# Maxima in query tiles of 112 rows, one transpose per group, and fewer second-chunk products in a three-attention decoder layer

## The reference, cut to what matters

```python
def attention(q, k, v, causal):            # 16 heads of 32
    scores = einsum('bhqd,bhkd->bhqk', q, k) / sqrt(32)
    if causal:
        scores = where(tril(ones((S, S))), scores, -inf)
    return einsum('bhqk,bhkd->bhqd', softmax(scores, axis=-1), v)

x = layernorm(x + lora_linear(attention(q(x), k(x), v(x), causal=True), wo))
h = ln(x + attention(q(x), k(x), v(x), causal=False))
h = ln(h + attention(q(h), k(ctx), v(ctx), causal=False))
x = layernorm(x + ln(h + ffn(h)))
x = layernorm(x + bit_ffn(x))
```

## Time and profile before

| | |
|---|---|
| median of three runs | 3351.85 us (3346.13 to 3355.16) |
| the profiled execution, first to last instruction | 3352.8 us |
| mean granted TensorE clock | 0.976 |
| PE busy | 3122.7 us (93%), 35500 matmuls |
| DVE busy | 2591.0 us (77%) |
| ACT busy | 2018.2 us (60%) |
| POOL busy | 1227.7 us (37%) |
| DMA | 405.71 MB, 44.5% of the 16 DMA engines' time |

### The profile page before, as it was taken

The page is one execution under the profiler, slowest core; times in us unless marked ns, Lnnn a source line. Parts: engine busy times, 40 slices in busy tenths (PEclk is TensorE's granted clock), DMA queues, the critical chain, the costliest instruction groups (busy, mean ns, idle before and its releaser), DMA issues.

```text
span 3352.8 us, 88599 instructions
## 1 busy us (share of the span) xinstructions
PE 3122.7 (93%) x35500; PEld 2438.7 (73%) x35500; DVE 2591.0 (77%) x4691; ACT 2018.2 (60%) x4586; POOL 1227.7 (37%) x1128
## 2 busy tenths in 40 slices
PE   6998999999999968999999999999979999999996
PEld 4888888878889846777777777777765656565562
DVE  5777788878889757888888888888855666666666
ACT  2665556656677636777777777777763544434342
POOL 0444431126665643344444443434113212222222
PEclk9999999999999988999999999999989999999998
DMA  3566654436554545656556545555342121121212
GB/s 101 161 192 208 193 167 142 147 118 189 173 165 136 162 113 123 140 132 138 133 123 138 135 124 139 128 135 113 87 173 76 45 53 44 50 54 50 55 38 48
DMA packets 445189, 405.71 MB, mean 121 GB/s; under 512 B 270471, under 2 KB 352523, under 8 KB 443630
## 3 DMA queue, kind: packets, MB, share of 16 engines
q1 hardware_dynamic: 444526, 399.78, 44.5%
q10 hardware_dynamic: 256, 0.26, 0.0%
HBM read 239.72 MB, written 109.52 MB: 104 GB/s over the span
## 4 chain that ended last, share of the span: by engine, by line
PE 59%; DMA 13%; DVE 12%; SPq 6%; ACT 5%; issue 3%; POOL 2%; ACTq 0%; POOLq 0%; DVEq 0%
PE at_ps L752 26%; PE at_ps L876 5%; PE at_ps L896 5%; PE at_ps L839 4%; PE at_ps L1404 4%; PE at_ps L1418 3%; DMA causal_spill<-at_proj 3%; PE at_ps L1429 3%; PE at_ps L1383 3%; DMA self_spill<-at_proj 2%; DVE at_mx_cross L964 2%; PE at_ps L781 2%; DMA at_o_raw<-at_values 2%; PE at_ps L851 2%; SPq L708 1%
## 5 line engine op out<-in xcount | busy, mean ns | idle before, releaser
L971 DVE TENSOR_TENSOR at_p<-at_ps,at_p 125x448 f16<-125x448 f32 (+1 forms) x1280 | 779.6, 617 | 167.5 <-ACT at_ps L924 158.6
L923 ACT ACTIVATE at_p<-at_ps 125x448 f16<-125x448 f32 (+1 forms) x1280 | 698.8, 546 | 292.8 <-PE at_ps L876 254.2
L924 ACT ACTIVATE at_ps<-at_ps 125x448 f32<-125x448 f32 (+1 forms) x1280 | 699.4, 546 | 0.0
L964 DVE TENSOR_REDUCE at_mx_cross<-at_ps 128x1 f32<-128x750 f32 x512 | 477.2, 932 | 41.1 <-PE at_ps L839 38.3
L1044 POOL TENSOR_TENSOR at_o_sum<-at_o_raw 128x256 f32<-128x256 f32 x192 | 121.3, 632 | 930.6 <-ACT at_o_raw L930 930.4
L876 PE MATMUL at_ps<-at_stacks 97*112 97x224 f16 (+2 forms) x1792 | 324.6, 257 | 23.2 <-DMA at_stacks<-at_mrow 19.2
L896 PE MATMUL at_ps<-at_values,at_p 112*128 112x33 f16 (+3 forms) x7168 | 317.0, 185 | 12.1 <-ACT at_o_raw L930 6.7
L916 ACT ACTIVATE at_proj<-at_ps 128x448 f16<-128x448 f32 (+2 forms) x320 | 155.1, 485 | 273.7 <-PE at_ps L752 273.2
L1383 PE MATMUL at_ps<-at_xt,at_early 128*128 128x256 f16 x1792 | 303.2, 276 | 7.8 <-ACT at_w_first L1453 4.9
L1452 ACT ACTIVATE at_masks<-at_ps,at_b_cols 128x256 f32<-128x256 f32 x224 | 107.2, 479 | 336.1 <-PE at_ps L1383 336.0
L967 DVE TENSOR_REDUCE at_mx<-at_ps 128x2 f32<-128x448 f32 x512 | 304.4, 610 | 5.7 <-PE at_ps L851 4.0
(11 more groups left out here) (203 smaller groups left out, 6775.6 us busy)
## 6 DMA issues: line engine op xcount, KB each, us to landing
at_x_res<-x SPq DMA_DIRECT2D x124, 256.0 KB, 3.1
cross_spill<-at_proj SPq DMA_DIRECT2D x64, 487.0 KB, 3.1
at_x_rows<-x SPq DMA_DIRECT2D x92, 256.0 KB, 4.5
at_prep<-bit SPq DMA_DIRECT2D x32, 512.0 KB, 4.6
at_early<-ctx SPq DMA_DIRECT2D x32, 512.0 KB, 5.1
at_stacks<-cross_spill SPq DMA_DIRECT2D x64, 243.5 KB, 3.7
causal_spill<-at_proj SPq DMA_DIRECT2D x64, 224.0 KB, 2.0
at_stacks<-causal_spill SPq DMA_DIRECT2D x128, 112.0 KB, 2.3
```

The costliest lines, as they stand in the source:

```text
L923: act.activation(mem.p_hi[0:self.KC, n % 4, :], scores, ACT.Exp, scale=EXP_SCALE)
L924: act.activation(scores, scores, ACT.Exp, scale=EXP_SCALE).then_inc(self.exp_done, 1)
L964: dve.tensor_reduce(self.mx[:, at, t, h:h + 1], mem.ps_qk[:, :, 0:self.KT // 2], AX.XY, ALU.max).then_inc(self.max_done, 1)
L971: dve.tensor_tensor(mem.p_lo[0:self.KC, n % 4, :], mem.ps_st[0:self.KC, self.st_bank(b, g, n), 0:2 * T], mem.p_hi[0:self.KC, n % 4, :], AL ...
```

## The change

Query tiles of the maxima are 112 rows (`QR`), without overlap, in all three attentions. A group's maxima, 112 rows by two tiles by four heads, are turned round by one transpose to eight rows, and `mrow` becomes eight partitions of 112; two DMAs, one for each tile, write the row, so the waits on `mrow_in` count 32. In the causal attention the first maximum tile needs 112 keys, and its other 112 columns are filled with a mask only in the first use of each of the two banks. In causal `scores` the second chunk is computed for the last 128 queries alone, so the exponentials and the subtraction run over 352 columns instead of 448, and `values` leaves out the second chunk for the first query tile. All products left out are with keys that the mask makes zero. The mask for the maxima is one triangle of 112 instead of two tiles.

```diff
--- before.py
+++ after.py
@@ -34,6 +34,7 @@
 GH = P // HD
 G = D // P
 TILES = (0, T - P)
+QR = T // 2
 S_ACT = 16.0
 S_W = 256.0
 UNSPLIT = 1.0 / (S_ACT * S_W)
@@ -338,7 +339,7 @@
         small = masks[:, :].bitcast(F16)
         self.ot = small[:, 0:1792].rearrange("p (i c t) -> p i c t", i=2, c=DC)
         self.mask_eye = small[:, 1792:1920]
-        self.mask_q = small[:, 1920:2368].rearrange("p (t k) -> p t k", t=2)
+        self.mask_q = small[:, 1920:2144]
         self.mask_k = small[0:T // 2, 2368:2816].rearrange("p (c k) -> p c k", c=2)
         self.ct = [space.bitcast(F16).rearrange("p (i c k) -> p i c k", i=2, c=DC)
                    for space in (masks[:, 0:4 * KT_PAD], second[:, 0:4 * KT_PAD])]
@@ -370,7 +371,7 @@
         self.yn_flat = sb("yn", [P, 2 * D])
         self.z, self.yn, self.y = sb("z", [P, 2, D]), self.yn_flat[:, :].rearrange("p (t d) -> p t d", t=2), sb("y", [P, 2, D])
         self.mx = [sb("mx", [P, 6, 2, GH]), sb("mx_cross", [P, 4, 2, GH])]
-        self.mrow = sb("mrow", [GH, 2, T], F16)
+        self.mrow = sb("mrow", [2 * GH, 2, QR], F16)
         self.stats, self.mv = sb("stats", [P, 2, 6]), sb("mv", [P, 2, 2])
         self.ve, self.rstd = sb("ve", [P, 2]), sb("rstd", [P, 2])
         self.neghalf = sb("neghalf", [P, 2])
@@ -463,6 +464,7 @@
         self.QTILES = (2 if self.cross else 1) * GH
         self.PAIRS = self.NCH // 2 * GH
         self.HALF = self.PAIRS // 2
+        self.P_COLS = T + P if self.causal else 2 * T
         self.w_part = mem.weights[index]
         self.stacks, self.values = (mem.cross_stacks, mem.cross_values) if self.cross else (mem.stacks, mem.values)
         self.RING = len(self.stacks)
@@ -711,7 +713,9 @@
             sp.dma_start(to[0:HD, :, T:], heads[:, :, T:width]).then_inc(self.stacked[g % 2], 16)
         elif kind == "row":
             sp.wait_ge(*self.released(kind, b, g))
-            sp.dma_start(self.qs(b, g)[96:97], self.mrow[:, g % 2, :]).then_inc(self.mrow_in[g % 2], 16)
+            for t in range(2):
+                sp.dma_start(self.qs(b, g)[96:97, :, t * QR:(t + 1) * QR], self.mrow[t * GH:(t + 1) * GH, g % 2, :]
+                             ).then_inc(self.mrow_in[g % 2], 16)
         elif kind == "store":
             if self.norm is None:
                 sp.wait_ge(self.yn_done, 2 * b + 2)
@@ -806,9 +810,8 @@
                                                      for t, q0 in enumerate(TILES)])
             elif kind == "row":
                 pe.wait_ge(self.max_done, self.tile(b, g, QTILES))
-                for t, q0 in enumerate(TILES):
-                    last = pe.transpose(mem.ps_proj[0:GH, bank, q0:q0 + P], self.mx[:, self.place(b, g), t, :],
-                                        mem.ident[:, :])
+                last = pe.transpose(mem.ps_proj[0:2 * GH, bank, 0:QR],
+                                    self.mx[0:QR, self.place(b, g), :, :].rearrange("p t h -> p (t h)"), mem.ident[0:QR, 0:QR])
             elif kind in ("y0", "y1"):
                 if b == self.b0:
                     pe.wait_ge(self.first_weights.w_lo_done, 8)
@@ -836,48 +839,43 @@
             if self.cross:
                 h, t = n // 2, n % 2
                 for half in range(2):
-                    last = pe.matmul(mem.ps_qk[:, half, 0:KT // 2], qs[0:96, h, TILES[t]:TILES[t] + P],
+                    last = pe.matmul(mem.ps_qk[0:QR, half, 0:KT // 2], qs[0:96, h, t * QR:(t + 1) * QR],
                                      ks[0:96, h, half * KT // 2:(half + 1) * KT // 2], start=True, stop=True)
             else:
                 wait(pe, self.max_done, self.tile(b, g, n) - 1)
+                bank = mem.ps_qk[0:QR, n % 2, 0:2 * T].rearrange("p (t k) -> p t k", t=2)
+                if self.causal and b == self.b0 and g == 0 and n < 2:
+                    pe.matmul(bank[:, 0, QR:T], mem.mask_eye[:, 0:QR], mem.mask_q[:, QR:T], start=True, stop=True)
                 for t in range(2):
 
-
-                    first = self.causal and t == 0
-                    k0, k1 = (0, T) if not self.causal or t else (0, P)
-                    if first:
-                        pe.matmul(mem.ps_qk[:, n % 2, 0:T], mem.mask_eye, mem.mask_q[:, 0, :],
-                                  start=True, stop=False)
-                    last = pe.matmul(mem.ps_qk[:, n % 2, t * T + k0:t * T + k1],
-                                     qs[0:96, n, TILES[t]:TILES[t] + P], ks[0:96, n, k0:k1],
-                                     start=not first, stop=not self.causal or first)
-                    if self.causal and not first:
-                        last = pe.matmul(mem.ps_qk[:, n % 2, t * T + TILES[t]:t * T + T], mem.mask_eye,
-                                         mem.mask_q[:, t, TILES[t]:T], start=False, stop=True)
+                    keys = QR if self.causal and t == 0 else T
+                    last = pe.matmul(bank[:, t, 0:keys], qs[0:96, n, t * QR:(t + 1) * QR], ks[0:96, n, 0:keys],
+                                     start=True, stop=not self.causal)
+                    if self.causal:
+                        last = pe.matmul(bank[:, t, t * QR:(t + 1) * QR], mem.mask_eye[:, 0:QR], mem.mask_q[:, 0:QR],
+                                         start=False, stop=True)
             last.then_inc(self.qk_full, 1)
         elif kind == "scores":
             qs, ks = self.qs(b, g), self.ks(b, g)
             if n == 0:
-                pe.wait_ge(self.mrow_in[g % 2], 16 * ((G * b + g) // 2 + 1))
+                pe.wait_ge(self.mrow_in[g % 2], 32 * ((G * b + g) // 2 + 1))
                 if self.cross and b == self.b0:
                     pe.wait_ge(self.slots_set, 2 * g + 2)
             m = self.pair(b, g, n)
             wait(pe, self.lo_done, m - ST_RING + 1)
             bank = self.st_bank(b, g, n)
             h, c0 = n // (NCH // 2), 2 * (n % (NCH // 2))
-            for c in (c0, c0 + 1):
-
-
-                first = self.causal and c > 0
-                q0, at = (c * KC if self.causal else 0), (c - c0) * T
-                if first:
-                    pe.matmul(mem.ps_st[0:KC, bank, at:at + T], mem.mask_eye[0:KC, 0:KC], mem.mask_k[:, c, :],
-                              start=True, stop=False)
-                last = pe.matmul(mem.ps_st[0:KC, bank, at + q0:at + T], ks[:, h, c * KC:(c + 1) * KC],
-                                 qs[:, h, q0:T], start=not first, stop=not self.causal or first)
-                if self.causal and not first:
-                    last = pe.matmul(mem.ps_st[0:KC, bank, at:at + KC], mem.mask_eye[0:KC, 0:KC],
-                                     mem.mask_k[:, c, 0:KC], start=False, stop=True)
+            if self.causal:
+                early, late = mem.ps_st[0:KC, bank, 0:T], mem.ps_st[0:KC, bank, T:T + P]
+                pe.matmul(early, ks[:, h, 0:KC], qs[:, h, 0:T], start=True, stop=False)
+                pe.matmul(early[:, 0:KC], mem.mask_eye[0:KC, 0:KC], mem.mask_k[:, 0, 0:KC], start=False, stop=True)
+                pe.matmul(late, mem.mask_eye[0:KC, 0:KC], mem.mask_k[:, 1, T - P:T], start=True, stop=False)
+                last = pe.matmul(late[:, P - KC:P], ks[:, h, KC:T], qs[:, h, KC:T], start=False, stop=True)
+            else:
+                for c in (c0, c0 + 1):
+                    at = (c - c0) * T
+                    last = pe.matmul(mem.ps_st[0:KC, bank, at:at + T], ks[:, h, c * KC:(c + 1) * KC], qs[:, h, 0:T],
+                                     start=True, stop=True)
             last.then_inc(self.st_full, 1)
         elif kind == "values":
             vs = self.vs(b, g)
@@ -890,6 +888,10 @@
             for c in (c0, c0 + 1):
                 for t, q0 in enumerate(TILES):
                     at = (c - c0) * T + q0
+                    if self.causal and c == 1:
+                        if t == 0:
+                            continue
+                        at = T
                     both = [(mem.p_hi[0:KC, n % 4, at:at + P], VW), (mem.p_lo[0:KC, n % 4, at:at + P], HD + 1)]
                     for k, (left, cols) in enumerate(both if c == 0 else both[::-1]):
                         at_h = h % 2 * VW
@@ -906,8 +908,8 @@
             return
         if kind in self.ALL_JOBS and self.by_scalar(kind):
             act.wait_ge(self.proj_full, self.full_index[kind, b, g] + 1)
-            wait(act, self.mrow_in[g % 2], 16 * ((G * b + g) // 2))
-            act.activation(self.mrow[:, g % 2, :], mem.ps_proj[0:GH, self.jobs.bank(kind, b, g), 0:T], ACT.Copy, bias=LIFT,
+            wait(act, self.mrow_in[g % 2], 32 * ((G * b + g) // 2))
+            act.activation(self.mrow[:, g % 2, :], mem.ps_proj[0:2 * GH, self.jobs.bank(kind, b, g), 0:QR], ACT.Copy, bias=LIFT,
                            scale=-1.0 / S_QK).then_inc(self.proj_hi, 1)
         elif kind in self.ALL_JOBS and kind not in self.UNSPLIT_JOBS:
             if kind[0] in "qk" and kind == self.first_stacked(b, g):
@@ -919,8 +921,8 @@
             m = self.pair(b, g, n)
             act.wait_ge(self.st_full, m + 1)
```

(23 more changed lines are left out.)

## The result

The changed kernel is slower: 3374.3 us, median of 8 runs (3363.4 to 3381.7), against 3352.1 us for the kernel before, measured beside it. The ratio of the times, with its 95% interval, is 1.0058 [1.0042, 1.0074]; the two medians alone would give 1.0066. The prediction was 3333 us, faster, in a range of 3300 to 3350. Its profiled execution took 3366.3 us, with a span of 3364.4 against 3352.8.

A forecast was written before the change was run, and what follows sets the result against it. SP's queue and DMAs were taken to bound causal batches 2 to 9, TensorE 450 to 690 us. Terms +3.4 - 2 - 16.4 + 1.6 - 6.4 = -19.8 took 3352.8 to 3333 us, range 3300 to 3350.

The forecast's parts named there:

- row transposes: All three attentions: one transpose instead of two saves TensorE 0.125 us a group, 24 us over 192 groups.
- TensorE's savings in its own stream: Causal attention, per head: maximum saves 0.055 us, scores 0.04, values 0.055; together 0.15 us.
- SP's queue counts everywhere: Rival, chance 0.13: both rows' second issues lengthen SP's chain, in every self batch too; 3358 us.
- There +0.6 - 0.125 - 0.1 = +0.37, and -0.5 in the other five: Self attention: 11 batches on SP's chain lose 0.37 us each, the other five gain 0.5; +1.6 us in all.
- Batches 2 to 9: Causal attention, 7.5 batches: SP's queue and DMAs set the period, 38.0 us between score tiles 0; +3.4 us.
- Net +0.45 x 7.5: Causal batches 2 to 9: 0.9 us more on SP, 0.46 less on TensorE's part of the chain; +3.4 us.
- Here 2.9 us each, less 0.3 for VectorE waits that stay: -16.4 us: Causal attention, 450 to 690 us, 6.3 batches: TensorE sets the pace, so its saved work shortens the run by 16.4 us.
- -6.4 us of the cross attention: Cross attention: 16 batches at 0.5 us saved make 8 us, 80% of it taken because VectorE is busy 88%.
- the clock case: Rival, chance 0.09: longer gaps in causal and self attention halve TensorE's clock; twelve falls at 2.6 us, 3364 us.
- a granted clock below 0.95 in the first stretch: Sign for the clock case: granted clock of 160 to 440 us falls from 0.99 to under 0.95.
- against it: Objection to the clock case: in SP's stretch a slow TensorE has the gaps' slack, save in 7.4 us a batch.
- Weight loads: Rival, chance 0.03: 2560 longer 112-column loads in all three attentions show, 33 ns each, +84 us; 3417 us.

The follow-up runs named there:

- e18: The changed kernel, unaltered, profiled a second time: 3371.0 us.
- e1: The changed kernel with the maxima row as before (two transposes into four rows of 224, one row DMA): 3352.3 us, ratio 0.9993 to the kernel before.
- e2: The kernel before with only its row DMA cut into two of 112 columns: 3372.4 us, ratio 1.0063.
- e9: The kernel before plus one small DMA a group on SP, half a row's size, behind the group's stack, to an unread buffer: 3371.1 us, ratio 1.0066.
- e6: The changed kernel with the causal load moved early, behind group 0's second exponential: 3362.2 us, ratio 1.0032 to the kernel before.
- e5: e1 with the causal load moved early, behind group 0's second exponential: 3338.2 us, ratio 0.9966 to the kernel before.
- e3: The changed kernel plus 24 overwritten matmuls ahead of the input-row wait in causal batches 3 to 12: 3368.9 us, ratio 1.0059 to the kernel before.
- e14: e1 plus 24 overwritten matmuls ahead of the input-row wait in causal batches 3 to 12: 3354.7 us, ratio 0.9995 to the kernel before.
- e13: e6 with residual and load of the self attention's group 0 moved behind its stack: 3405.9 us, ratio 1.0176 to the kernel before.
- e11: e5 with residual and load of the self attention's group 0 moved behind its stack: 3388.9 us, ratio 1.0122 to the kernel before.
- e4: The kernel before with only the causal attention's smaller second key chunk; 128-row tiles, two transposes, one row DMA stay: 3349.9 us, ratio 0.9980.
- e7: The kernel before with only the causal load moved early, behind group 0's second exponential: 3343.9 us, ratio 0.9972.
- e15: e4 with the causal load moved early, behind group 0's second exponential: 3342.3 us, ratio 0.9953 to the kernel before.
- e8: The changed kernel with both row DMAs issued from ScalarE's queue instead of SP's: 3552.3 us, ratio 1.0603 to the kernel before.

## Why the prediction was wrong, point by point

**The sum and what was measured** (first profile of the change, and e18):

| stretch | forecast | measured |
|---|---|---|
| causal batches 0 to 9 | +3.4 - 2 = +1.4 | +15.9, +13.1 |
| causal batches 10 to 15 | -16.4 | -6.1, -3.2 |
| self attention | +1.6 | +4.6, +7.7 |
| cross attention | -6.4 | -4.7, -0.9 |

In parts, by the ratios: the forecast gave the smaller chunk and the 112-row tiles (e1) -17.8 us (-2.6, -2, -13.2, and nothing in self and cross), the row transposes and the smaller eviction some -15.4, the second DMA +13.4. Measured are -0.07% or -2 us for e1, 0.63% or +21 for the second DMA (e2), and no gain from the transposes, since the change lies 0.65% over e1. Of the 39 us between -19.8 and +19, then, some 31 are work that TensorE really was rid of and that the kernel's time did not show, and 8 are the price of the DMA; each ratio is uncertain by some 5 us. The three steps below are of both kinds.

**What held.** TensorE's savings in its own stream, to 0.02 us, and the row's eviction (366 to 252 ns, 0.1 us forecast). That batches 2 to 9 hang on SP's queue and the DMAs behind it: the mean distance of their score tiles 0 grew from 39.0 to 40.4 us, and the waits for input rows and row in 160 to 440 us rose from 18.7 to 31.3 us (some 40 were forecast). Of all cases the rival "SP's queue counts everywhere", given 0.13, came nearest: it had both rows on the chain of all 16 self batches. Its total, 3358 us, was still 16 short.

**The first step that failed, which set the sign: "There +0.6 - 0.125 - 0.1 = +0.37, and -0.5 in the other five".** I counted one issue of 0.6 us, in the 11 batches with a wait for stacks. e2, e9 and e6 (against e5) put one more DMA a group at 15.5, 14.1 and 15.1 us of the self attention: 0.9 to 1.0 us in each of the 15 distances between its batches, one and a half issues of the earlier trace rows. The 11 waits were those that the trace shows, not the batches that hang on the chain; with a little more on SP there were 15 to 19. In all it costs 0.5 to 0.7%, 17 to 23 us (alone in e2 and e9; together with the single transpose in the change against e1, e6 against e5, e3 against e14 and e13 against e11), where my terms for it came to 7.5 x 0.9 + 11 x 0.6 = 13. The change's own profiles show less of it in the self attention (2.2 and 5.3 us over e1) and more in batches 10 to 15 (4.8 and 7.7), which cost e2 nothing: there e2 still had TensorE as its bound (223.8 us with and without the DMA), and the change no longer has. The first of them is also an execution 8 us quicker than the median.

**The second: "Batches 2 to 9", "Net +0.45 x 7.5".** The second row's part was near enough (+0.9 x 7.5, some +7, forecast; +3.8 by e2). What I left out is that TensorE's saving could make the stretch longer: e4 and e1, without the row DMA, are 13.8 and 8.7 us longer in this stretch. The distance of an average batch from its score tile 0 to the first product of the input rows (the mean over batches 2 to 9 but 6, which has a pause of its own) rises from 19.35 to 20.03 us in e4, and from the issue of the last of their loads to their use are 6.03 us instead of 5.18. The rest of the batch, from there to the next score tile 0, grows as well, from 18.47 to 19.10, so the late rows are only half of the 1.3 us a batch. While the rows and the weight piece are under way in one batch (403.9 to 409.4 us before, 412.2 to 419.7 in e4) the DMA engines do this, DMA share and GB/s last:

```profile
403.90:409.40 5.50, 4.78 (x85) 4.59 (x82) 4.54 (x9) 4.81 (x12) 1.47 (x2) 1.00 1.00 363
```

```profile
412.20:419.70 7.50, 4.92 (x84) 4.77 (x81) 5.96 (x13) 5.44 (x14) 1.11 (x2) 0.94 0.88 289
```

The rows come later although nothing was added to any queue; this pair of batches is farther apart than the average pair. With the weight piece and the rows no longer issued together (e7, e15, e5) the stretch is equally long in all three, so the loss comes only where they fall together. Why it comes when TensorE has less to do is open: an order of arrivals, I take it, but no run shows it.

**The third: "Here 2.9 us each, less 0.3 for VectorE waits that stay: -16.4 us".** The stretch without SP's chain gained 10.9 us in e1 (37.3 to 35.5 us a batch) and 6.1 or 3.2 in the change, where 13.2 and 16.4 were forecast for 6.3 batches: TensorE's new waits there are for the input rows as well as for VectorE. TensorE's waits in 490 to 700 us of the changed kernel:

```profile
PE at_ps L747 <- DMA at_x_rows<-x: 7.0, 4, 2.5
PE at_ps L813 <- DVE at_mx L969: 4.0, 5, 0.8
```

The terms for the row transposes, "-0.5 in the other five" and the -6.4 us of the cross attention among them, brought nothing in sum either. No run takes them apart, so why stays open.

**Clock.** The sign set for the clock case was a granted clock below 0.95 in the first stretch. It came to 0.93, and the case was wrong all the same: e3 and e14 give most of the clock back (0.93 to 0.98 and 0.95 to 0.98) and the time stays. Its "against it" was right, the slow TensorE has slack. A sign chosen for a rival has to be one that the rival alone can give.

**Weight loads.** 0.03 was fair for the size, not for the thing. They are 129 ns instead of 98 throughout the cross attention. The line's forms in the change (ns: min/median/max) and in the kernel before:

```profile
L842 PEld LDWEIGHTS at_ps<-at_stacks x512: 126/129/213, 1289.8 to 2482.4; 96*112 96x112 f16 x171
```

```profile
L839 PEld LDWEIGHTS at_ps<-at_stacks x512: 95/98/152, 1273.8 to 2471.0; 96*128 96x128 f16 x171
```

The mean time from the start of such a maximum's matmul to TensorE's next, over 920 starts in 1300 to 2400 us, rose from 166.3 to 176.0 ns. Most of it lies between the two products of one maximum: their median distance rose from 163 to 178 ns without a wait ahead of them and from 170 to 203 behind one. That is 8 to 10 us over the cross attention, over a quarter of the 32 us that 1024 loads add there, and more than the 6.4 us of gain that I gave it. The stage's length is 1317.8 us on average in ten profiles with 128-row tiles there and 1320.7 in nine with 112 (e8 left out), single profiles 1311 to 1325, so the loss is suggested there, not shown. The Trainium skill (TensorE: Matmul & The Clock Gate, weight-path perf modes) has the fast load at 128 weights only; the load's own length agrees. In the causal attention, where the median maximum took the 0.25 to 0.26 us expected, it stayed hidden, and in the self attention the mean distance of a maximum's products rose by 7 ns: of all three attentions' 79 us some 10 showed, not the third that the rival needed.

## What to carry to other kernels

Where a written order of issues on one queue sets the period, count DMAs before matmuls: here one small DMA a group cost 0.65% at either of two places, while 38 to 62 us of TensorE's work brought nothing clear of noise. Before taking work off an engine, take the same amount of wait off the chain, by trial: moving one load and one residual in the written order gave 0.75% with all the work kept. Visible waits are a lower bound of the steps that hang on a chain; count the steps that have the same structure, not those that happened to wait.

## What the runs showed of the hardware that was not expected

- Small DMAs add up. A row's takes 0.58 us of SP's queue, 0.62 to the next (876.05 to 876.68 in e2), the added one of e9 0.34. One more a group cost 0.63 and 0.66%, most of it in the self attention (15.5 and 14.1 us for 60 of them, some 0.25 us each) and nothing in causal batches 10 to 15 (223.8 us in both).
- Issued from ScalarE instead of SP, two such DMAs a group cost 5.4% (e8 against the change).
- Half-clock time of TensorE, 24 to 38 us of it less, changed nothing where the chain runs over SP (e3, e14).
- A stretch with less TensorE work was longer by 9 to 14 us, when the load of a weight piece and that of the input rows were in flight together (e1, e4).
- Loads of 112 columns of weights take 129 ns where those of 128 columns take 98. Between the two 375-column products of a maximum this shows in part: the second starts 15 ns later in the median without a wait ahead, 33 ns later behind one. In the causal attention it doesn't show.
